# Two attention cores of an eight-stage transformer kernel: scores on half rows in the full core, on whole rows in the causal core

## The reference

```python
# layer 1: every query sees every key
energy = jnp.einsum('bqhd,bkhd->bhqk', q, k)
attn = jax.nn.softmax(energy / jnp.sqrt(jnp.float32(D)), axis=-1)
out = jnp.einsum('bhqk,bkhd->bqhd', attn, v).reshape(B, S, D)
...
# layer 2: silu projections, scales per head, a lower triangle
scores = jnp.where(mask, scores, -jnp.inf)
probs = jax.nn.softmax(scores, axis=-1)
out = jnp.einsum('bhnm,bhmd->bhnd', probs, v)
```

## Time and profile before

| | us |
|---|---|
| median of 3 runs | 3366.22 |
| profiled execution, own time | 3390.4 |
| its span, first to last instruction | 3388.6 |
| full core (first product to last copy) | 774.4 |
| causal core | 516.9 |

### The profile page before, as it was taken

One profiled execution on the slowest core, in us unless ns is written; L12 is line 12 of the kernel. 1 busy time (PEld: TensorE's weight loads), 2 busy tenths in 40 slices (PEclk: granted clock), 3 DMA queues, 4 the chain that ended last, 5 costly groups with the idle time before them and its releaser, 6 DMA issues. The chain is left out here.

```text
span 3388.6 us, 46001 instructions
## 1 busy us (share of the span) xinstructions
PE 2548.5 (75%) x16517; PEld 1212.2 (36%) x16545; DVE 2007.4 (59%) x3056; ACT 1514.8 (45%) x3024; POOL 563.7 (17%) x860
## 2 busy tenths in 40 slices
PE   2998533379999999939984899999567676575578
PEld 1775222212222222226762233332336335343423
DVE  3553478588888888431123777774565484447655
ACT  1332221137777777723331466666255255432211
POOL 3000012000000000000001111111274074203145
PEclk8998656669999999969996799998789798887679
DMA  2111000111111111010001111110100000000000
GB/s 69 46 48 37 3 6 0 57 42 41 42 38 37 36 35 41 3 61 6 1 1 60 59 60 59 58 58 18 41 15 2 14 30 5 8 5 2 1 19 13
DMA packets 62158, 99.70 MB, mean 29 GB/s; under 512 B 23946, under 2 KB 36396, under 8 KB 61548
## 3 DMA queue, kind: packets, MB, share of 16 engines
q1 hardware_dynamic: 61932, 96.75, 8.9%
HBM read 82.10 MB, written 14.02 MB: 28 GB/s over the span
## 5 line engine op out<-in xcount | busy, mean ns | idle before, releaser
L930 DVE TENSOR_REDUCE l1a_core_mpart<-l1a_core_psA 128x1 f32<-128x1024 f32 x512 | 602.1, 1219 | 125.7 <-PE l1a_core_psA L835 123.5
L908 ACT ACTIVATE l1a_core_prob<-l1a_core_psB 128x512 f32<-128x512 f32 x1024 | 548.1, 600 | 238.3 <-PE l1a_core_psB L851 231.4
L930 DVE TENSOR_REDUCE l2a_core_mpart<-l2a_core_psA 128x1 f32<-128x1024 f32 (+7 forms) x384 | 335.0, 909 | 141.3 <-PE l2a_core_psA L839 71.3
L908 ACT ACTIVATE l2a_core_prob<-l2a_core_psB 128x512 f32<-128x512 f32 (+3 forms) x640 | 313.6, 533 | 213.9 <-PE l2a_core_psB L851 206.8
L851 PE MATMUL l1a_core_psB<-l1a_core_qh,l1a_core_kh 75*128 75x512 bf16 x1024 | 337.8, 390 | 7.4 <-ACT l1a_core_prob L908 7.4
L867 PE MATMUL l1a_core_psV<-l1a_core_prob,l1a_core_vh 128*32 128x512 f32 x2048 | 275.3, 610 | 7.1 <-ACT l1a_core_oh L898 6.4
L835 PE MATMUL l1a_core_psA<-l1a_core_ka,l1a_core_qa 64*128 64x512 bf16 x1024 | 209.2, 406 | 55.2 <-DMA l1a_core_ka<-kparts 31.9
L867 PE MATMUL l2a_core_psV<-l2a_core_prob,l2a_core_vh 128*32 128x128 f32 (+3 forms) x1856 | 195.5, 445 | 19.5 <-POOL l2a_core_prob L793 15.7
L851 PE MATMUL l2a_core_psB<-l2a_core_qh,l2a_core_kh 75*128 75x256 bf16 (+3 forms) x928 | 201.2, 304 | 3.5 <-DMA l2a_core_qh<-l2a_core_mT 2.4
L851 PEld LDWEIGHTS l1a_core_psB<-l1a_core_qh,l1a_core_kh 75*128 75x128 bf16 x1024 | 78.2, 97 | 264.0 <-ACT l1a_core_prob L908 168.0
L1609 DVE SCALAR_TENSOR_TENSOR X<-l1e_psO,W,X 128x128 f32<-128x128 f32 x128 | 36.0, 344 | 220.6 <-PE l1e_psO L1566 220.6
(11 more groups left out here) (630 smaller groups left out, 4436.0 us busy)
## 6 DMA issues: line engine op xcount, KB each, us to landing
l1a_core_qa<-qparts SPq DMA_DIRECT2D x64, 96.0 KB
l1a_core_ka<-kparts SPq DMA_DIRECT2D x32, 192.0 KB
l2a_core_qa<-qparts SPq DMA_DIRECT2D x64, 96.0 KB
l2a_core_ka<-kparts SPq DMA_DIRECT2D x32, 192.0 KB
l0a_core_kh<-kparts SPq DMA_DIRECT2D x48, 96.0 KB
l0a_core_qh<-qparts SPq DMA_DIRECT2D x48, 96.0 KB
l1a_core_qh<-qparts SPq DMA_DIRECT2D x48, 96.0 KB
l1a_core_kh<-kparts SPq DMA_DIRECT2D x16, 288.0 KB
```

What stands on the lines that cost most here:

```text
L908: nc.scalar.activation(prob[n % RING][:, 0:cols], psB[n % 3][:, 0:cols], ACT.Exp, scale=scale).then_inc(b_exped, 1)
L930: ins = nc.vector.tensor_reduce(mpart[:, place, part:part + 1], psA[i % 2][:, lo * P:hi * P], AX.X, ALU.max)
```

## The change

The shared function is split in two.

**Full core** (`wide_attention_core`). The second scores no longer use 75 rows in one product. `main_terms` does the 64 rows of `ka`/`qa`, and `tail_terms` adds, into the same bank, another 64 rows (`kt`/`qt`: the ninth term, the three rows of maxima, and rows that contribute nothing). Every score product of the core, first or second, now stands on half of the rows. `kt` and `qt` are also kept twice, so `load_m` issues six DMAs. Four units of second scores with their slots are written out by hand for each block of keys:

**Causal core** (`causal_attention_core`). `qa` and `ka` and their loads are gone; the first scores are products over all 72 rows of `qh`/`kh`, one after the other:

```diff
-                for e, at, place, kb, nb in products:
-                    rows = slice(64 * e, 64 * e + 64)
-                    ins = mm(ps[:, at * P:(at + nb) * P], qa[h % 2][rows, place * P:(place + 1) * P],
-                             ka[h % 2][rows, kb * P:(kb + nb) * P], start=True, stop=at + nb - 1 not in masked,
+                for at, place, kb, nb in products:
+                    ins = mm(ps[:, at * P:(at + nb) * P], qh[h % 3][0:QK_ROWS, place * P:(place + 1) * P],
+                             kh[h % 3][0:QK_ROWS, kb * P:(kb + nb) * P], start=True, stop=at + nb - 1 not in masked,
                              skip_group_check=True)
```

```diff
-            units[-1].append((used, kb, 4 * c + first, nb))
+            if runs and runs[-1][1] == first and (4 - first) * (runs[-1][2] + 1) <= 4:
+                runs[-1][2] += 1
+            else:
+                runs.append([c, first, 1])
...
-            load_a(0)
             load_b(0)
-            load_a(1)
             load_b(1)
+            load_b(2)
             load_m(0)
```

More of the change, by code:

```diff
@@ L613, in maxima_plan @@
     for pair in pairs:
-        products = [(e, 4 * e, place, kb, nb) for e, (place, kb, nb) in enumerate(pair)]
+        products = [(4 * e, place, kb, nb) for e, (place, kb, nb) in enumerate(pair)]
         (p0, k0, n0), (p1, k1, n1) = pair
@@ L620, in maxima_plan @@
             seen[place] += 1
-        masked = [at + nb - 1 for e, at, place, kb, nb in products
-                  if kind == "causal" and kb + nb - 1 == query_block(kind, place)]
+        masked = [at + nb - 1 for at, place, kb, nb in products if kb + nb - 1 == query_block("causal", place)]
         units.append((products, maxima, masked))
@@ L697, in attention_core2 @@
     for u, pieces in enumerate(b_units):
-        for at, kb, place, nb in pieces:
-            if kind == "causal" and query_block(kind, place) == kb:
-                diagonal[u] = diagonal.get(u, []) + [at]
+        for at, kb, c, first, groups in pieces:
+            if c <= kb % 4 < c + groups and first == kb // 4:
+                diagonal.setdefault(u, []).append(at + (kb % 4 - c) * (4 - first))
     ND = sum(len(x) for x in diagonal.values())
@@ L706, in _ @@
         def _(sp):
[L707 to L714, removed]
-                        sp.dma_start(qa[b][lo:lo + nj * HD, :], g.qparts[i:i + 1, heads, :]
-                                     .broadcast_to([nj, HD, S])).then_inc(qa_loaded[b], 16)
-                    sp.dma_start(ka[b][copy:copy + 6 * HD, :], g.kparts[h:h + 1].broadcast_to([2, 3 * HD, S])).then_inc(qa_loaded[b], 16)
-                    sp.dma_start(ka[b][copy + 6 * HD:copy + 8 * HD, :], g.kparts[h, 0:2 * HD]).then_inc(qa_loaded[b], 16)
             def load_b(h):
@@ L863, in values @@
                 for u, pieces in enumerate(b_units):
-                    for at, row, place, nb in pieces:
-                        if row == kb:
-                            c, lo = place // 4, place % 4 * P
-                            ins = mm(psV[32 * c:32 * c + 32, lo:lo + nb * P], vh[h % 2][:, kb, :],
-                                     prob[(NB * h + u) % RING][:, at * P:(at + nb) * P], start=kb == 0,
-                                     stop=kb == (12 + c if kind == "causal" else NT - 1), skip_group_check=True)
+                    for at, row, c, first, groups in pieces:
+                        for i in range(groups if row == kb else 0):
+                            lo = at + i * (4 - first)
+                            ins = mm(psV[32 * (c + i):32 * (c + i) + 32, first * P:CH], vh[h % 2][:, kb, :],
+                                     prob[(NB * h + u) % RING][:, lo * P:(lo + 4 - first) * P], start=kb == 0,
+                                     stop=kb == 12 + c + i, skip_group_check=True)
                 ins.then_inc(pv_done, 1)
```

278 lines of the change are left out of this document (256 added, 22 removed).

## The result

The changed kernel takes **3390.47 us** (median of 20 runs, 3371.56 to 3404.09); the kernel before, measured beside it, 3370.27 (20 runs). The ratio is 1.0054, interval 1.0036 to 1.0071: slower by 0.5%, about +18 us (+12 to +24) on the 3366 us of the forecast, which said +9.

What follows compares the result with a forecast made beforehand. The prediction took PE to bound both cores. Full core +29 us and causal core -20 us gave +9 us on the 3366.22 us median, so 3375 us, own range 3350 to 3402.

Steps and rivals of the forecast that it cites:

- Full core, forecast +29: Full core: a bank wait of 0.435 us eats the 0.44 saved per block; +29 us, from +16 to +46.
- forecast +7: Last head of the full core, without slots: a block takes 2.83 us instead of 2.39, +7 us.
- The +2 for three more DMAs: Full core's start: three more DMAs for the maxima, 0.61 us each, delay the first second score by +2 us.
- Blocks 1, 14 and 15: Full core: the three key blocks of a head that differ from the ordinary 2.83 us; put at 3.28, 3.00 and longer.
- The wait of the third slot: Full core, block 15: the third slot waits for the first slot's `psA` buffer; about 0.8 us idle a head, ended by DVE.
- Causal core, forecast -20: Causal core: -6 us at the start, -8 from POOL's order, -6 from shapes against columns; range -8 to -33.
- Order on POOL: Causal core: zeroing key block 7 before splitting the maxima shortens a 1.12 us wait; -0.55 us a head, between 0 and -1.12.
- Changes of shape against columns: Causal core: whole rows save 3.6 us of shape changes, unpaired products cost 3.2 us; net -0.4 us a head.
- 1 (no bank wait, 3284): Full core: shape changes were the bound and the bank wait does not bite; block 2.40 us, total 3284; 10%.
- 2 (weight loads of the second pass not hidden, block 3.03): Full core: a pass behind one on its own half costs 0.32 us instead of 0.215; +51 us, total 3426; 5%.
- 3 (halves side by side only in one unit): Full core: halves share the array only within one unit; block 3.7 us, +220 us, total 3595; 4%.
- 4 (full costs less, causal gives more): Both cores: POOL wait goes altogether, third slot hidden; +16 - 28 = -12 us, 3354, up to 3366; 16%.

Runs made afterwards that it cites:

- experiment 4: Changed kernel with four banks for second scores and three single banks for first scores, each reduced by itself: ratio 1.0085 to the kernel before.
- experiment 7: Changed kernel with every exponential of the full core covering only 256 of 512 columns: ratio 0.9906 to the kernel before.
- experiment 5: Changed kernel with four banks for second scores, three single ones for first scores, and first scores spread through the block: ratio 0.9852, 3324.56 us.
- 6: The kernel before, unedited, timed and profiled once more: ratio 0.998 to itself.
- experiment 10: The changed kernel, unedited, timed and profiled once more: ratio 1.0056 to the kernel before.
- experiment 11: Kernel before with the changed causal core and POOL's split of the maxima at unit 31: ratio 0.9948 to the kernel before.
- experiment 1: Kernel before with only the full core changed, causal core as before: ratio 1.0087, +29 us.
- experiment 8: Changed kernel with POOL's split of the maxima one unit earlier, at 28, in the causal core: ratio 1.0523 to the kernel before.
- experiments 3: Changed kernel with the third slot of the full core's last key block moved behind the last two tails: ratio 1.0029 to the kernel before.

## Why the prediction was right, and where it was not

**Sign and mechanism.** The forecast was likeliest (65%), and its mechanism is what happened: the half rows save their changes of shape, and the wait of `main_terms(u+3)` for the bank of u eats them. Shown by experiment 4 in the last head (the same passes with a fourth bank, 2.40 in place of 2.82), by experiment 7 in all heads (the same passes with a shorter exponential, 2.61), and by experiment 5, where the saving comes out. One of the signs named was not to be seen, an idle time of 0.2 us before the second L775: the second does start 0.41 late, but the profile models the first as busy until 0.04 before it.

**Full core, forecast +29.** By parts, from the second profiles (6 against 10): start to the first copy of the maxima -0.4; from there to the sixteenth copy +18.1 (forecast +20 and +2: 46.73 - 45.44 = 1.29 a head as forecast, but in thirteen intervals, the first and the last being +0.3 and +0.95); from there to the end +8.35 (forecast +7: fourteen blocks of the last head at 2.82 instead of 2.40 and a longer block 1, less 1.0 at its very end, make +5.1; the other 3.2 lie ahead of its block 1, where the last blocks of the fifteenth head have no slots either, and which the forecast counted as ordinary blocks). Together +26; timed alone +29. The +2 for three more DMAs was nearly right: the first second score comes 5.2 us after the first copy of the maxima instead of 3.75, and waits 1.41 of them for a DMA into `qt`; the first interval is only 0.3 longer all the same. Blocks 1, 14 and 15 took 3.36, 2.98 and 3.70; forecast 3.28, 3.00 and 3.68. The wait of the third slot is 0.92 and is ended by DVE, as told.

**Causal core, forecast -20: the step that failed, by its size.** The start was right: -6. The heads were put at -0.4 and -0.55, -0.95 together, and measured -0.56, so 8 us of the 14. What they were made of:

- Order on POOL: -0.55. 1.12 became 0.67, -0.45. "0.5 to 0.6 of the wait stays" was about 0.1 us too little. That the rest of the wait is worth its full length, experiment 11 shows.
- Copy of `psV`, which the forecast kept as it was in the causal core: 0.25 us of waiting before, 0.34 now, +0.1 a head.
- Changes of shape against columns: -0.4. What is left of -0.56 is about -0.2. Not tried apart, so how it divides between changes and columns stays open.

Two things have no term in the forecast. In the fourth and the ninth head of the changed kernel the first of the second scores waits for a DMA of the maxima, 0.7 to 1.1 us, which makes these heads 30.0 to 30.4 us long; the granted clock is 1.00 there. First profile, timeline:

```profile
1990.70 0.39 PE L1121 MATMUL l2a_core_psB<-l2a_core_qh,l2a_core_kh 75*128 75x512 bf16 x1 [1.05 <-DMA l2a_core_qh<-l2a_core_mT]
```

The forecast worked out the margin of these DMAs in the full core and not here. In the kernel before such heads are longer by up to 0.6. Why the DMA lands late in some heads and not in others stays open. And ahead of the last head PE waits 2.46 us for POOL's split, 1.62 before (last section).

Timed alone the causal core gave -6 (-14 to +1), less than the -13 of its stretches, which lies near the end of that interval. Experiment 11 is short by about as much: timed -17 (-24 to -11), by its stretches about -23. The difference between the two timings, 11 us, is the 15 heads at 0.74. So the 6 to 8 us by which both timings fall short of the stretches may be noise, or something that the stretches do not hold; this stays open.

**The sum.** By stretches it is +26 - 13 = +13, near the forecast of +9. The spans say nothing as fine: those of the same two profiles are 3399.3 and 3377.0, +22.3, of which 7.5 lie ahead of the full core, where both kernels are the same, and those of the first two differ by -17. Timed twice it was +18 and +19. The causal heads explain 6 of the missing 9 or 10. As for the rest, the full core's +29 of experiment 1 is 3 more than its stretches; such differences are of the size by which the kernel before differs from itself, and stay open. That +9 lies as near as it does is not luck by terms that cancel: the full core's terms came out within 3 us, and the miss is the causal core's.

**Rivals.** 1 (no bank wait, 3284): ruled out by the row that is 0.80 us long. 2 (weight loads of the second pass not hidden, block 3.03): ruled out, passes on one half follow at 0.22 (1013.69, 1013.92, 1014.13, 1014.35). The held against it lie at the granted clock 0.50, so they were weaker evidence than this. Here the measurement goes against the sentence of the Trainium skill (TensorE: Matmul & The Clock Gate, "Part 3: Packing small matmuls") by which only a load into another row group would overlap. The same section also lets a load into the background weight buffer go ahead, and the 0.22 us agrees with that. 3 (halves side by side only in one unit): ruled out by the four pairs. 4 (full costs less, causal gives more): neither; the third slot did wait, and the wait on POOL did not go.

## What to carry to other kernels

Making an engine's instructions cheaper pays only when its buffers turn at the new pace: with n banks, unit u+n can't start earlier than one product, one exponential and their signals after unit u, and putting units together at the end of a block uses up the spacing that hid it. Work that round trip out for the new order, and look for it in a stretch of the old trace where nothing else stands in between (here the last head). When a bank is moved from one ring of buffers to another, the order has to be moved with it: four banks gave +0.9% in the changed kernel's order and -1.5% in a new one, both with the changed causal core.

## What the runs showed of the hardware that was not expected

- **A short idle time can cost far more than itself, and need not.** In experiment 8 an idle time of PE of 2.43 us in each head went with 24 us at the granted clock 0.50, and a head took 11.8 us more. With 1.12 us at a like place or 0.67 after the change, heads kept their pace (29.72 and 29.16). So the changed kernel's order on POOL was worth 12 us a head by comparison with the old split point in the new order, though only 0.45 by comparison with the kernel before.
- **The same idle time did not always bring the lower clock.** Ahead of the last causal head PE waits for the last step of POOL's split, 2.46 us in every profile of the changed causal core. Timeline and busy time by stretch, first profile of the changed kernel, then experiment 10:

```profile
2336.63 0.22 PE L1097 MATMUL l2a_core_psA<-identb,l2a_core_mb 128*128 128x128 bf16 x1 [2.46 <-POOL l2a_core_mb L1057]
2336.90:2367.20 30.30, 27.24 (x230) 8.24 (x229) 0.20 (x1) 23.24 (x51) 6.65 (x23) 1.00 0.02 4
```

```profile
2340.51 0.22 PE L1097 MATMUL l2a_core_psA<-identb,l2a_core_mb 128*128 128x128 bf16 x1 [2.46 <-POOL l2a_core_mb L1057]
2340.80:2384.70 43.90, 43.00 (x229) 9.92 (x229) 0.18 (x1) 23.33 (x52) 6.69 (x23) 0.57 0.01 3
```

The same work took 30.3 us and 43.9. It ran at 1.00 in the profiles of the changed kernel and of experiments 3 and 7, and at 0.57 to 0.63 in all others, the three with the old causal core among them, where the wait is 1.62 us. So the length of the idle time alone does not decide it; what does was not tried. That one place moves a whole execution by 0.3 to 0.4%. This is why single profiled executions are no measure of a 0.5% difference, and heads of equal clock are.

- **Half-row products of unrelated groups run together.** Second scores and first scores, into different banks, from different operands, started within 0.01 us of each other.
